# Later scalar copies, an earlier up product and an eighth unit transposed by halves in a two-layer transformer kernel

## The reference

```
sim = jnp.einsum('bwie,bwje->bwij', bq, bk)      # 8 heads of 64, windows of 128, masked
attn = jax.nn.softmax(sim, axis=-1)
out = jnp.einsum('bwij,bwje->bwie', attn, bv)
```

## Time and profile before

| | us |
|---|---|
| median of 3 runs | 966.91 (966.57 to 967.67) |
| the profiled execution | 964.24 |
| its span in the trace | 963.0 |
| PE busy in the span | 922.3 |
| DVE, ACT, POOL busy | 658.3, 506.4, 437.1 |

### The profile page before, as it was taken

One profiled execution on the slowest core, in us unless ns is written; L12 is line 12 of the kernel. 1 busy time (PEld: TensorE's weight loads), 2 busy tenths in 40 slices (PEclk: granted clock), 3 DMA queues, 4 the chain that ended last, 5 costly groups with the idle time before them and its releaser, 6 DMA issues. The chain is left out here.

```text
span 963.0 us, 14392 instructions
## 1 busy us (share of the span) xinstructions
PE 922.3 (96%) x4904; PEld 613.7 (64%) x4904; DVE 658.3 (68%) x1584; ACT 506.4 (53%) x1168; POOL 437.1 (45%) x351
## 2 busy tenths in 40 slices
PE   5899999999999999999899998999989999999998
PEld 3555566676566766677566766667656676557765
DVE  5957868687675885758766677757777477624933
ACT  3664784536746276462854538445474454735222
POOL 6859236651094401863036620566206541055443
DMA  7050310611323132130232302332033220433071
GB/s 287 8 181 1 123 45 2 143 45 40 108 66 97 25 100 62 53 98 23 100 70 75 89 1 100 72 95 68 1 100 91 70 62 2 135 76 88 23 166 34
DMA packets 41753, 72.86 MB, mean 76 GB/s; under 512 B 11984, under 2 KB 13008, under 8 KB 41296
## 3 DMA queue, kind: packets, MB, share of 16 engines
q1 hardware_dynamic: 40112, 69.81, 26.4%
q10 hardware_dynamic: 1568, 2.13, 0.6%
HBM read 69.04 MB, written 2.88 MB: 75 GB/s over the span
## 5 line engine op out<-in xcount | busy, mean ns | idle before, releaser
L1173 ACT ACTIVATE wide<-ps 128x512 f32<-128x512 f32 x136 | 81.1, 596 | 211.2 <-PE ps L511 210.6
L1105 ACT ACTIVATE pw<-ps,w_cols 128x512 f32<-128x512 f32 x144 | 98.8, 688 | 103.6 <-PE ps L511 102.9
L1947 POOL TENSOR_TENSOR atc<-atc,wide 128x512 f32<-128x512 f32 x64 | 82.1, 1284 | 117.9 <-DVE atc L1651 117.9
L665 PE MATMUL ps<-pw,w_w 128*128 128x512 f32 x288 | 135.4, 592 | 0.0
L1065 ACT ACTIVATE pw<-ps,nmax 128x256 f32<-128x256 f32 x256 | 118.3, 480 | 24.2 <-DVE nmax L1423 19.7
L1927 POOL TENSOR_TENSOR kr<-qks,w_rope 128x512 f32<-128x512 f32 x32 | 43.7, 1366 | 144.5 <-DVE qks L1401 144.2
L509 PE MATMUL ps<-yc,eg 128*128 128x512 f32 x128 | 94.3, 737 | 0.0
L1947 POOL TENSOR_TENSOR pt<-pt,wide 128x512 f32<-128x512 f32 x48 | 61.7, 1286 | 66.8 <-DVE pt L1651 66.8
L1423 DVE TENSOR_REDUCE nmax<-ps 128x4 f32<-128x1024 f32 (+1 forms) x80 | 78.4, 997 | 8.2 <-PE ps L571 7.9
L665 PEld LDWEIGHTS ps<-pw,w_w 128*128 128x128 f32 x288 | 53.6, 189 | 43.2 <-issue 38.2
L509 PE MATMUL ps<-yc,w 128*128 128x512 f32 x144 | 79.5, 552 | 1.3 <-ACT pw L1105 1.3
(11 more groups left out here) (231 smaller groups left out, 2138.9 us busy)
## 6 DMA issues: line engine op xcount, KB each, us to landing
wb<-scratch SPq DMA_DIRECT2D x128, 256.0 KB, 4.0
wb<-scratch SPq DMA_DIRECT2D x32, 512.0 KB, 5.9
wide<-scratch SPq DMA_DIRECT2D x16, 512.0 KB, 6.0
xin<-in_x SPq DMA_DIRECT2D x8, 256.0 KB, 3.0
out<-wide SPq DMA_DIRECT2D x7, 256.0 KB, 2.1
wb<-in_w SPq DMA_DIRECT2D x1, 1152.0 KB, 8.5
w_w<-in_w SPq DMA_DIRECT2D x1, 1152.0 KB, 12.3
w_ed<-in_ed SPq DMA_DIRECT2D x1, 1024.0 KB, 15.7
```

What stands on the lines that cost most here:

```text
L665: pe.matmul(bank(k), w2[:, e, c, :], hid[:, n % 4, :], start=c == 0, stop=c == 1 and e < E0).then_inc(*DOWN0.one)
L1105: act.activation(hid[:, n % 4, :], bank(UPS0[n % 2]), ACT.Gelu, bias=cols[:, C_B1 + 2 * e + c:C_B1 + 2 * e + c + 1], scale=1.0).then_inc(* ...
L1173: act.activation(sgl[:, (c + 1) % 3, :], bank(UPS1[2 * ((c + 1) % 2)]), ACT.Silu).then_inc(*SILU.one)
L1947: pool.tensor_tensor(hh[h], hh[h], sgl[:, (c + 1) % 3, :], ALU.mult).then_inc(*HH_POOL.one)
```

## The change

Three edits, all for steps 2 to 7.

1. ACT, `attention`: the copy of bank 7 of units 2, 4 and 6 (`pt_copy_half(s, u - 1, 1)`) moves from between `exps(s, u, 0)` and `exps(s, u, 1)` to behind `exps(s, u, 1)`.
2. PE, `attention`: the first up product (E0/0) moves from behind turn 6 to ahead of it.
3. PE and DVE: unit 7 is turned by `turn_by_halves` in place of two `turn` calls, and DVE copies it with `pt_copy_half`.

```
                     for u in range(1, UNITS - 1):
                         if u > 1 and u % G == 1:
                             weigh_pair(s, u // G - 1)
+                        if u == UNITS - 2:
+                            up0_half(s, E0, 0)
                         turn_by_halves(s, u)
                         if u + 3 < UNITS:
                             scores(s, u + 3)
-                    up0_half(s, E0, 0)
                     weigh_pair(s, PAIRS - 2)
-                    turn(s, 7, 0)
-                    turn(s, 7, 1)
+                    turn_by_halves(s, 7)
                     up0_half(s, E0, 1)
...
                     exps(s, u, 0)
-                    if halved_by_scalar(s, u - 1):
-                        pt_copy_half(s, u - 1, 1)
                     if u == 3 and second:
...
                     exps(s, u, 1)
+                    if halved_by_scalar(s, u - 1):
+                        pt_copy_half(s, u - 1, 1)
                     if u in (4, 6) and s > 1:
...
                     for u in range(UNITS):
-                        copied = pt_copy_half if u < UNITS - 1 else pt_copy
                         if u + 2 < UNITS:
                             maxima(s, u + 2)
-                        copied(s, u, 0)
+                        pt_copy_half(s, u, 0)
                         if not halved_by_scalar(s, u):
-                            copied(s, u, 1)
+                            pt_copy_half(s, u, 1)
                         invert(s, u)
```

## The result

The changed kernel takes 958.61 us (median of 4 executions, 958.30 to 958.66), the kernel before in the same comparison 967.11. The ratio is 0.991, with a 95% interval of 0.989 to 0.993. The gain is 8.5 us.

The account below looks back on a forecast made before the run. PE was taken as the bound, busy 922.3 of 963.0 us. Savings of 0.86 + 0.21 = 1.07 us in six steps made 6.4 us, taken from the median 966.91: 960.5 us, range 959.0 to 963.6.

Parts of the forecast that it names:

- The up product ahead of turn 6: PE, steps 2 to 7: the product fits the idle time before turn 6; that wait shrinks from 1.43 to about 0.5 us.
- Turn 6 to weigh pair 2: PE: the weigh starts 0.68 us after turn 6, not 1.54, so it comes 0.86 us earlier a step (0.79 to 0.99).
- Turn 7 by halves: PE: sixteen small transpositions replace eight large ones, 0.64 us instead of 0.85, saving 0.21 us a step.
- Weigh pair 3 and DVE: DVE's copies of unit 7 finish in time for weigh pair 3 on PE, with a margin of 0.08 us.
- ACT's copies: ACT: copying behind both exponentials buys nothing by itself, but up to 0.3 us behind the other two edits through an earlier GELU.
- The sum: Whole kernel: 0.86 + 0.21 = 1.07 us in each of six steps, 6.4 us in all.
- The step that failed: Whole kernel: the profiled 964.24 us was 2.67 under the median 966.91, so the gain was taken from the median, giving 960.5.
- new wait: Rival: weigh pair 3 waits for DVE or turn 7 for ACT; 3.4 to 5.2 us of gain remain; chance 0.17.
- dearer change of form: Rival: PE's tile form changes at turns 6 and 7 cost 0.2 us more each, 2.4 in all, 962.9; chance 0.05.
- given back later: Rival: PE leaves the attention 1.07 us earlier but waits as long later, 966.9 us; chance 0.05.
- ACT's copies are not late: Denies the rival that ACT's late copies delay three turns a step, 970.4 us at a slip of 2.45; chance 0.03.
- the drains: PE: by the skill's rule, changing tiling mode drains TensorE; form changes rise from five to seven, yet the sum stays 6.4 us.

Follow-up runs that it names:

- experiment 5: Kernel before, plus a spare product, overwritten unread, in PE's idle time ahead of turn 6: 964.98 us (ratio 0.9973), kernel before beside it 967.61.
- experiments 3 to 6: Changed kernel with ACT's old order 960.64 us; changed kernel unedited 958.12; kernel before with long wait filled 964.98; changed kernel with a step 0 wait filled 958.60.
- experiment 7: Kernel before, unchanged, traced twice more: 965.76 us and 967.74 us, both at a mean clock of 0.996.

## Why the prediction was right in the steps and wrong in the time

- *The up product ahead of turn 6.* Right. It lies in the idle time, and the wait is 0.49 (forecast 0.5). The waits for DVE's copies fell to 10.2 us (forecast 10.5).
- *Turn 6 to weigh pair 2.* I took 0.68 for the distance, and it is 0.64: the gain of this part was 0.90, and 0.86 was 0.04 a step too small. It is the same as with an up product behind the turn.
- *Turn 7 by halves.* Forecast 0.21, and the timeline has 0.21 (0.85 to 0.64). Alone, it measured 1.2 us.
- *Weigh pair 3 and DVE.* The margin of 0.08 held: no trace with the half turn has a wait for DVE there.
- *ACT's copies.* That they buy nothing alone held (ratio 1.0003). Behind the other edits I gave them up to 0.3 a step, and they are worth 0.45. That estimate was a third too small: in the old order the first GELU holds PE up more than the prediction had it, the up product alone gives 3.5 to 3.9 us, and the three edits alone add up to 3.9 + 1.2 + 0 = 5.1 at most where together they give 6.9. It does not touch the sum, which has the three together.
- *The sum.* 1.07 a step forecast, 1.146 measured. 0.04 of the difference is the weigh above; another 0.04 is between turns 5 and 6, 2.14 us before and 2.10 now, which I had held fixed. The spare product of experiment 5 has the same 2.10, so it comes with a product ahead of turn 6; why it does is not shown. It makes 6.9 us in place of 6.4.
- *The step that failed* is the last of the sum: "that execution was 2.67 us under the median of 966.91, so I take the difference from the median". I treated the 2.67 us as an offset that both kernels have. They are the price of the clock's falls. The profiled execution had none; one fall of the usual length takes about 0.002 from the mean clock, and the others lost up to three times that (0.994). Where the dear ones lie was seen in two traces: behind the wait of 1.43 us ahead of turn 6, which the change cuts to 0.49. A third trace has its falls in step 0 alone, where the change alters nothing. Filling the wait alone, in another set of executions, takes back 2.6 us. So the 967.11 of the kernel before is 964.5 and 2.6 of clock, and the 958.61 of the changed one is 964.5 − 6.9 = 957.6 and about 1.0 that lies ahead of step 2 (0.88 in its first trace, with the fall in step 0, and 0.71 in its second, without it). The 8.5 us are 6.9 of waits and work and 1.6 of clock, less what the start of the program lost; no execution near the median of this comparison has a trace, so that split is worked out and not read. Of the 2.1 us by which the forecast missed the gain, 0.5 are the terms above, with which the sum would have given 960.0, inside the range; the 1.6 are this step. They are no constant either: in the set of experiments 3 to 6 the medians are 967.61 and 958.12, a gain of 9.5. Made against the profiled execution, the sum gave 957.8, and a profiled execution of the changed kernel took 958.30.
- *The rivals.* None came: no new wait, no dearer change of form, nothing given back later, and ACT's copies are not late. Turn 6 to weigh and turn 7 to up product are 0.64 us each. That the drains of the Trainium skill's "TensorEngine Tiling (Array Packing)", Key Properties, would not change the sum agrees with that.

What stays open is why the clock falls at some of these waits and not at others of the same length. In the second trace of experiment 7 it fell behind two of six. Nor was anything run that gives or takes only the falls in step 0.

## What to carry to other kernels

Before setting a profiled execution against a median, look at the granted clock of several executions. If the clocks differ, the distance between the two can be a cost with a place in the trace, and a change at that place moves it. An idle stretch of the busiest engine can cost more than its length: 1.43 us of waiting cost another 1.6 each time that the clock fell behind it, and a spare product in it paid for itself. And an edit that is worth nothing alone can be worth more than a third of the whole behind the others (2.7 of 6.9 us here), so the edits of a change are also to be measured left out one at a time.

## What the runs showed of the hardware

PE's granted clock fell to its lower level behind a wait as short as 1.43 us, after three others of 0.32, 0.59 and 0.30 us in the 14 us ahead of it, in an engine that was busy for 96% of the span. That fall came in 3 of 36 such waits. The kernel before had a clock under 1.000 in all 14 executions timed beside the kernel with the long wait filled, and that kernel in 4 of 9. The Trainium skill, "TensorE: Matmul & The Clock Gate", section "A second HAM failure mode: psum-queue depth-cycling", tells of a kernel whose PE idles briefly and often between groups of matmuls and loses clock by it. The windows of steps 2, 3 and 7 agree in this, that the clock is lower behind short waits (0.72 and 0.76); there the waits came between groups all the time, here the fall follows the longest.

A fall in step 0 is cheaper. It made the turns of step 0 take 1.14 us longer (29.46 for 28.32), while the waits among the later of these turns shrank from 1.95 us to 1.60, and less than that arrives at the end: the changed kernel took 958.30 in the execution with this fall and 958.25 in the one without it. In the steps 2 to 7, where PE sets the time, a fall costs 1.6 us.
